# A two-layer cross-attention and expert kernel: first-layer experts on the whole array, second-attention scores in quarter arrays without spread queries, deeper rings for the scatters

## The reference

```python
x = x + xattn0(layernorm(x), ctx)            # 8 heads of 64, over the channels
x = x + ffn0(layernorm(x))                   # 16 experts, inner 64, top 2, and a shared expert
x = x + xattn1(layernorm(x), ctx, mask)      # 16 heads of 16
x = x + ffn1(layernorm(x))                   # 32 experts, inner 128, top 4

# ffn0, for the two chosen experts of a token
hmid = silu(x @ w1[e].T) * (x @ w3[e].T);   y += weight[e] * hmid @ w2[e].T
# xattn1
scores = clip(einsum('bhsd,bhtd->bhst', q, k) / 4, -50, 50)    # head h reads channels 16h to 16h+15
probs = softmax(where(mask, scores, -50));  ctx_ = probs @ v
delta = rs * (ctx_ @ Wo.T + bo);            delta = layernorm(delta) * gamma + beta
```

## Time and profile before

| what | value |
|---|---|
| its own time | 1966.79 us |
| its span in the trace | 1965.1 us |
| busy: PE, DVE, ACT, POOL | 1618.1, 1468.4, 1014.1, 1131.1 us |
| mean granted TensorE clock | 0.915 |
| attention 0 | 0 to 830 us |
| shared expert | 830 to 983 us |
| experts 0 | 983 to 1141 us |
| combine 0 | 1141 to 1176 us |
| attention 1 | 1176 to 1617 us |
| experts 1 | 1617 to 1899 us |
| combine 1 | 1899 to 1965 us |

### The profile page before, as it was taken

One profiled execution on the slowest core, in us unless ns is written; L12 is line 12 of the kernel. 1 busy time (PEld: TensorE's weight loads), 2 busy tenths in 40 slices (PEclk: granted clock), 3 DMA queues, 4 the chain that ended last, 5 costly groups with the idle time before them and its releaser, 6 DMA issues. The chain is left out here.

```text
span 1965.1 us, 44433 instructions
## 1 busy us (share of the span) xinstructions
PE 1618.1 (82%) x15032; PEld 1194.9 (61%) x15032; DVE 1468.4 (75%) x3211; ACT 1014.1 (52%) x3084; POOL 1131.1 (58%) x1061
## 2 busy tenths in 40 slices
PE   4999999999999999799477707988887209999958
PEld 3677777777777777566255403544445109999846
DVE  2799999999999999757244455999998407888767
ACT  2788888888888888534143303333332006655520
POOL 2566666666666666536445503568788544666543
PEclk9999999999999999989788858999897559999979
DMA  6400000000000000022344350011112544555438
GB/s 180 141 18 18 18 18 18 18 18 18 18 18 18 18 18 18 35 87 80 114 149 149 104 190 14 12 47 68 67 47 79 212 165 134 161 162 157 155 131 321
DMA packets 101070, 167.71 MB, mean 85 GB/s; under 512 B 19999, under 2 KB 75756, under 8 KB 100208
## 3 DMA queue, kind: packets, MB, share of 16 engines
q1 hardware_dynamic: 75120, 105.37, 16.9%
q0 software_dynamic: 22272, 56.15, 7.9%
q10 hardware_dynamic: 3456, 3.34, 0.5%
HBM read 95.31 MB, written 75.76 MB: 87 GB/s over the span
## 5 line engine op out<-in xcount | busy, mean ns | idle before, releaser
L380 POOL TENSOR_TENSOR w_down<-w_down,attn_rsum 128x1024 f32<-128x1024 f32 x256 | 484.7, 1893 | 287.8 <-DVE attn_rsum L336 287.7
L296 ACT ACTIVATE w_down<-attn_ps_s,attn_negmax 128x256 f32<-128x256 f32 x1024 | 469.8, 476 | 25.6 <-DVE attn_negmax L330 22.5
L852 POOL DMA_INDIRECT l_by_token<-l_experts_outs,l_experts_rows x240 | 244.8, 1020 | 198.4 <-issue 107.8
L330 DVE TENSOR_REDUCE attn_negmax<-attn_ps_s 128x4 f32<-128x1024 f32 x256 | 311.9, 1218 | 28.2 <-PE attn_ps_s L218 27.4
L341 DVE COPY w_down<-attn_ps_t 128x1024 f32<-128x1024 f32 x256 | 312.1, 1219 | 21.0 <-PE attn_ps_t L230 20.7
L218 PE MATMUL attn_ps_s<-ctx_d,attn_q_sb 64*128 64x256 f32 x2048 | 273.6, 379 | 1.6 <-ACT w_down L296 1.0
L244 PE MATMUL attn_ps_qo<-w_down,attn_vb 128*64 128x256 f32 x2048 | 249.3, 385 | 1.3 <-DVE w_down L341 1.3
L716 PE MATMUL l_experts_ps_gu<-l_experts_rows_t,l_experts_w_now 128*128 128x128 f32 (+1 forms) x1920 | 213.6, 290 | 30.4 <-issue 14.6
L218 PEld LDWEIGHTS attn_ps_s<-ctx_d,attn_q_sb 64*128 64x128 f32 x2048 | 223.8, 189 | 3.1 <-issue 2.2
L716 PEld LDWEIGHTS l_experts_ps_gu<-l_experts_rows_t,l_experts_w_now 128*128 128x128 f32 (+1 forms) x1920 | 194.3, 183 | 41.8 <-issue 41.8
L296 ACT ACTIVATION_READ_ACCUMULATOR w_down<-attn_ps_s,attn_negmax 128x1 f32 x1024 | 213.9, 209 | 0.0
(11 more groups left out here) (247 smaller groups left out, 2670.7 us busy)
## 6 DMA issues: line engine op xcount, KB each, us to landing
l_experts_rows<-l_rows_in SPq DMA_DIRECT2D x240, 136.0 KB
combine_rows_got<-l_by_token SPq DMA_DIRECT2D x32, 512.0 KB
ctx_d<-in_ctx SPq DMA_DIRECT2D x64, 128.0 KB
combine_rows_got<-l_by_token SPq DMA_DIRECT2D x32, 256.0 KB, 3.8
w_gu<-in_w_gu SPq DMA_DIRECT2D x2, 4096.0 KB, 17.9
l_rows_in<-zeros SPq DMA_DIRECT2D x1, 4352.0 KB, 39.6
x_sb<-in_x SPq DMA_DIRECT2D x32, 128.0 KB
w_down<-in_w_down SPq DMA_DIRECT2D x1, 4096.0 KB, 12.6
```

The lines of the kernel that those rows point to most:

```text
L296: last = nc.scalar.activation(prob[:, n % 4, c, :], ps_s[:, n % 2, c, :], ACT.Exp, bias=negmax[:, n % 2, c:c + 1], accum_out=sums[:, n % 2 ...
L330: nc.vector.tensor_reduce(negmax[:, n % 2, :], ps_s[:, n % 2, :, :], AX.X, ALU.max, negate=True).then_inc(max_ready, 1)
L380: nc.gpsimd.tensor_tensor(prob[:, n % 4, :, :], prob[:, n % 4, :, :], rsum[:, n % 2, :].unsqueeze(2).to_broadcast([P, 4, A_N]), ALU.mult). ...
L852: pool.indirect_dma_start(m.by_token, bass.IndirectOffsetOnAxis(ap=place, axis=0), outs[:, r % RING, b, :], None, bounds_check=T * m.K - 1 ...
```

## The change

**Experts 0.** Gate and up of a block come from one product of 128 columns (gate in columns 0 to 63, up in 64 to 127): four products a pair instead of eight. The silu reads the gate half and writes rows 64 to 127 of `glu`; DVE's product becomes two operations of 64 rows. `w_down0` gets a second copy with zeros in the other half, so that `down` contracts all 128 rows; `copy_down` and its semaphore go, and PE picks the expert by a register, as in layer 1. Two memsets of the zero halves are added to the setup.

**Attention 1.** The spreads of DVE and POOL (L1422) and the copies of the mask row (L1653) go. ACT makes, once per group and half f, four masked copies of the projected queries (`take_apart`, `q_apart`): copy h keeps head h of each 64-row strip. The scores of a tile are eight products of 64 rows by 64 columns, 256 query columns each, in quarters of the array. `q_t` is single-buffered; `xa` and `xt` get their own memory.

**Scatters.** `Routing.RING = 4`: slots, semaphores and `xf` are rings of four, in the shared stage the slots too. In attention 1 POOL's order by j is (g-3, k=1), (g-4, k=3), (g-2, k=0), (g-3, k=2), over 46 steps.

```diff
-                for u in range(2):
-                    if HALVES == 2:
...
+                for u in range(2 // HALVES):
+                    for b in range(2):
                         for kt in range(KT):
+                            last = nc.tensor.matmul(ps_gu[:, q % 2, u, b, :], w_now[:, q % 2, b, kt, u * P:(u + 1) * P],
+                                                    rows_t[:, q % 2, b, kt, :], start=(kt == 0), stop=(kt == KT - 1))
...
+                    weights = w_down[:, b, bass.ds(e[b], 1), :] if HALVES == 2 else w_down[:, bass.ds(e[b], 1), :]
...
-                if HALVES == 2 and 0 <= n + 1 < NP:
-                    copy_down(n + 1)
...
             def scores(it, r):
                 keys_ready(pe, it, r // GT)
-                tdone(pe, qbd0_ready, it, r)
-                tdone(pe, qbd1_ready, it, r)
+                gdone(pe, q_apart_ready, it, r // GT)
                 tdone(pe, clip_ready, it, r - 1)
                 for f in range(KT):
...
+                    for strip in range(2):
+                        rows = slice(strip * S, (strip + 1) * S)
+                        for b in range(2):
+                            t0 = (r % GT) * P + b * S
+                            last = nc.tensor.matmul(ps_s[b * S:(b + 1) * S, strip, f * 256:(f + 1) * 256],
+                                                    k_t[rows, (r // GT) % 2, f, t0:t0 + S],
+                                                    q_apart[rows, (r // GT) % 2, f, :, t0:t0 + S], start=True, stop=True)
...
+            def take_apart(it, q, f, u, heads_of_strip):
+                use_done(act, bank_free, it, u)
+                if q >= 2:
                     tdone(act, s_made, it, (q - 1) * GT - 1)
...
+                for h in heads_of_strip:
+                    last = nc.scalar.activation(q_apart[:, q % 2, f, h, :], q_t[:, f, :], ACT.Copy, scale=w["strip_mask"][:, h:h + 1])
...
-                if texists(it, r + 2):
-                    spread_queries(it, r + 2)
...
-                q = g - 2 if j >= 2 else g - 3
+                if j == 2 and gexists(it, g - 4):
+                    rt.mark_sent(pool, it, g - 4)
+                q, k = ((g - 3, 1), (g - 4, 3), (g - 2, 0), (g - 3, 2))[j]
```

More of the change, by code:

```diff
@@ L797, in clip @@
                 last.then_inc(gu_used, 1)
-            experts_of = block_experts(mybir.EngineType.DVE) if HALVES == 2 else None
-            def copy_down(n):
-                e = experts_of(0, n)
-                done(dve, y_made, 0, n - RING)
-                for b in range(2):
-                    last = nc.vector.tensor_copy(down_now[half(b), n % RING, :],
-                                                 w_down[half(b), bass.ds(e[b], 1), :].rearrange("p a n -> p (a n)"))
-                last.then_inc(down_ready, 1)
             def product(n):
@@ L812, in product @@
                 if bias is None:
-                    nc.vector.tensor_tensor(act_t[:, n % RING, 0, :], glu[:, n % 2, 0, :], ps_gu[:, n % 2, 1, 0, :], ALU.mult)\
-                        .then_inc(a_ready, 1)
+                    for b in range(2):
+                        last = nc.vector.tensor_tensor(act_t[half(b), n % RING, 0, :], glu[I:P, n % 2, b, :],
+                                                       ps_gu[I:P, n % 2, 0, b, :], ALU.mult)
+                    last.then_inc(a_ready, 1)
                 else:
@@ L889, in __init__ @@
         self.steps = ph.sem("routing_steps")
-        self.scattered = [ph.sem("scattered0"), ph.sem("scattered1")]
+        self.scattered = [ph.sem(f"scattered{n}") for n in range(Routing.RING)]
         self.rows_sent = ph.sem("rows_sent")
@@ L899 @@
     STEPS = 8
+    RING = 4
     def step_done(self, dve, it, q, n):
@@ L1415, in _ @@
                 sp.dma_start(into, source).then_inc(later_written, 16)
-        def block_diagonal(engine, it, r, f, ready):
-            t0 = (r % GT) * P
-            for b in range(2):
-                source = q_t[:, (r // GT) % 2, f, t0 + b * S:t0 + (b + 1) * S]
-                last = engine.tensor_tensor(q_bd[:, r % 2, f, b, :, :], source.unsqueeze(1).to_broadcast([P, C_HALF, S]),
-                                            w["head_mask"][:, :].unsqueeze(2).to_broadcast([P, C_HALF, S]), ALU.mult)
-            last.then_inc(ready, 1)
         @block.tensor
@@ L1549, in _, with copy_queries, copy_keys @@
             act.wait_ge(opened, 1)
[L1551 removed]
+            def copy_queries(it, q, f, u):
                 use_done(act, bank_made, it, u)
[L1553 to L1558 removed]
+                gdone(act, q_apart_ready, it, q - 1)
+                nc.scalar.activation(q_t[:, f, :], ps_q[:, :], ACT.Identity, bias=w["bq"][:, f:f + 1],
+                                     scale=C_DH ** -0.5).then_inc(bank_free, 1)
+            def take_apart(it, q, f, u, heads_of_strip):
+                use_done(act, bank_free, it, u)
+                if q >= 2:
+                    tdone(act, s_made, it, (q - 1) * GT - 1)
+                for h in heads_of_strip:
+                    last = nc.scalar.activation(q_apart[:, q % 2, f, h, :], q_t[:, f, :], ACT.Copy, scale=w["strip_mask"][:, h:h + 1])
+                if f == KT - 1 and heads_of_strip[-1] == 3:
+                    last.then_inc(q_apart_ready, 1)
+            def copy_keys(it, q, f, u):
+                use_done(act, bank_made, it, u)
+                if q >= 2:
+                    tdone(act, s_made, it, (q - 1) * GT - 1)
+                nc.scalar.activation(k_t[:, q % 2, f, :], ps_q[:, :], ACT.Identity, bias=w["bk"][:, f:f + 1])\
+                    .then_inc(bank_free, 1)
             def copy_values(it, r, u):
@@ L1614, in step @@
                         rt.exponentials(act, it, g - 2, gdone)
+                    if j == 1 and gexists(it, g + 1):
+                        take_apart(it, g + 1, f, u + 1 + f, (0, 1))
+                    if j == 2 and gexists(it, g + 1):
+                        take_apart(it, g + 1, f, value_use(r - 1) + 1 + f, (2, 3))
             copy_transposed(0, 0, xt, xa_t_made, xt_ready, xt_reader)
             for f in range(KT):
-                copy_projected(0, 0, f, f - 6, q_t, w["bq"], C_DH ** -0.5)
+                copy_queries(0, 0, f, f - 6)
+            for f in range(KT):
+                take_apart(0, 0, f, f - 6, (0, 1, 2, 3))
             act.wait_ge(prepared, 2)
@@ L1789, in _ @@
                 deviation(0, q, vare_a, rstd_a, steps_a, xa_ready, rstd_a_ready)
-            spread_queries(0, 0)
-            spread_queries(0, 1)
-            for r in range(NT + 2 * GT + 2):
+            rounds = [qk for g in range(NG + 5) for qk in ((g - 3, 1), (g - 4, 3), (g - 2, 0), (g - 3, 2)) if 0 <= qk[0] < NG]
+            for r in range(NT + 3 * GT + 2):
                 step(0, r)
-            rt.mark_sent(pool, NG // 2 - 1, 1)
+            rt.mark_sent(pool, 0, NG - 1)
         def counts_final(pe):
```

139 lines of the change are left out of this document (52 added, 87 removed).

## The result

The changed kernel took 1892.65 us, the median of four executions (1887.08 to 1900.79), against 1969.03 us before (1962.18 to 1975.22): a ratio of 0.9604, 95% interval 0.9570 to 0.9637, 76 us less. The profiled execution has a span of 1885.3 us against 1965.1, 79.8 less.

What follows compares the result with a forecast made beforehand. DVE was taken to bound attention 1, in lock-step with POOL. Attention 1 -54.5, tail -10, experts 0 +3, shared stage -1.5 make -63 on 1966.8, giving 1904; two thirds of 6.6 toward the median gives 1908 us, range 1886 to 1942.

Steps and rivals of the forecast that it cites:

- The forecast's floor: Full group of attention 1: DVE's work left without spreads and mask copies, its own short waits staying: 31.8 us.
- the lock-step of DVE and POOL: Full group of attention 1: the two meet every step, so the larger of each step counts, summing to 34.0 us.
- Groups 0 and 1: First two groups of attention 1: -3 us from halved scores in group 0, -5 us in group 1.
- rival (a): Attention 1: meeting points, masked copies or non-overlapping quarters bind; six groups save 3 to 6 us; 1925 to 1950 us; 22%.
- signs of being wrong: Scores still 1.9 us, PE waiting on ACT's copies, clock 0.5 in attention 1, or POOL always waiting while DVE idles.
- Rival (d): Attention 1: halved scores make PE less dense and its clock falls low; some +118 us, 2090 us; 4%, slower.
- The tail: POOL's scatter turns behind attention 1's last tile: 86 us becomes 76, taken as -10, bounds +5 and -20.
- the stall of 8: POOL's tail in attention 1: the 14.0 us stall shrinks to about 8 as other groups' turns fill it.
- The prologue: Attention 1 ahead of the first clip: eight masked copies on ACT, between 0 and +5.5 us, +3.5 taken.
- The term for `down`: Experts 0: `down` on 128 rows costs 0.43 us more a pair, 17 us if PE set the pace, 2 charged.
- rival (b): Attention 1: DVE's stretch goes too, DVE at 31 us a group, tail -20; total 1875 to 1895 us; 15%.
- the signs named: Right if full groups 33 to 36 us, DVE 28 to 30, PE 30 to 31, ACT 25, tail 76, experts 0 unchanged.

## Why the prediction was right, and where its steps were not

**What bounds the kernel.** Right. That PE isn't the bound is shown: with only PE relieved the groups stay at 43.1 us and the ratio at 0.9992. That it is DVE, and POOL only behind it, rests on their waits in the trace, not on a run that relieves one of them.

**DVE in a full group.** The forecast's floor, 31.8 us, is what came (31.9). It then raised this to 34.0 by the lock-step of DVE and POOL, taking the larger of the two in each step. That step failed: the run with 0.57 us more on POOL in each step shows that POOL's time is mostly not passed on, 3.0 us over all groups for 18 added, though in groups 3 and 5 most of it was. That the floor was met to 0.1 us is in part luck: it took DVE's 2.8 idle us as staying, they became 3.4, and DVE's busy time fell by 11.7 where 11.2 was counted. Groups 2 to 5 gave 43.0 for 36, 7 of the 17 us by which the forecast missed the profiled gain of 79.8.

**Groups 0 and 1.** -14.3 for -8. For PE, halving the scores (7.75 us to 4.38 in each) explains 3.4 a group; the quarters with spreads took only 1.4 off group 0 and nothing off group 1. Group 1 gained 9.0, of which quarters make 3.4 (the run with halves) and the spreads' end 5.6. The forecast had counted PE's busy time in these groups as work, and some of it went away with the spreads. By what way isn't shown.

**ACT.** Two errors that cancelled. The forecast counted sixteen masked copies a group, 11.0 us; four copies of each of two halves are eight, 5.3 us. And it costed them at nothing because of holes of 1.3 us. At its own count that would have been wrong: the run with ACT at 24.0 us a group, the load that the forecast wrote down (24.9), lost 45 us in the groups. The bound that the forecast gave for it, 5.6 us a group, is what that run measured in the mean; the working behind it, four times 1.4, is another, and a part of the loss is the clock's, so the equality is luck. Had the code had sixteen, a result like that run's is likely: its ratio, 0.988, makes 1945 of the 1969 us before, in the range of rival (a). A wait of PE on ACT's copies, one of the signs of being wrong, did come, 4.5 us in the prologue.

**PE and its clock.** Scores of a tile took 1.09 us for 0.97: the quarters run side by side, as assumed. PE in a full group is 28.8 us where 30.8 was forecast: the granted clock is 1.00 in groups 3 to 5, where the earlier trace rows has 0.88 for group 4. Rival (d) had it the other way: PE was to be less dense with less work. It became denser, since the groups shrank by 26% and PE's work by less: 28.8 of 31.9 is 0.90, against 35.6 of 43.0, 0.83, part of it at the lower level. With quarters alone PE did become less dense, and the clock of groups 3 to 5 was 0.87 in the mean for 0.92. The observation of the rival was right, its sign here was not.

**The tail.** -4.7 from the last beta addition to the last issue (86.4 to 81.7) for -10; within the bounds. Twelve turns came, as counted, and the stall of 8 was 7.5. The miss is in the turns, 5.6 us each where 5.4 was taken, and in the other waits for landings, 5.9 us where 3 was. The stall itself was put down to the turns' own order, and it is the 8 MB weight load: 7.5 us in the changed kernel, 14.0 in the old order with rings of two or four, 0.4 at most at that place with the load in pieces. That it shrank as forecast doesn't show the forecast's reason.

**The prologue.** +4.8 for +3.5: the eight copies take 4.99 us and PE waits for the values behind them.

**Experts 0.** +3 was forecast, the traces say -2.0, and the comparison of the two forms on one chip says 0. The term for `down`, 0.43 us a pair more, was right in size (48.4 us for 40 pairs where the kernel before has 32.0: 0.41 more) and is hidden. What failed is the share of it that a row buffer's round trip was to pay.

**Shared stage.** -2.5 for -1.5. The wait of DVE on `rows_sent` is gone; the profile has no such row in this stage.

In sum: the direction, the bound and the place were right. The result of 1892.65 lies below the 1895 to 1925 that had 54%, in the 1875 to 1895 of rival (b), though not for all of its reasons: the full groups (31.9 for its 31) and the outer ones went its way, its tail of -20 did not. That the whole range of 1886 to 1942 was met owes something to errors of opposite sign: the forecast of the groups was 14 us too careful, that of the tail 5 too bold, experts 0 off by 3 to 5, and 4.7 of the profiled gain belong to attention 0, which didn't change. Of the signs named, the scores in about 1 us, DVE's 28 to 30 us and experts 0 came; the full groups (31.9 for 33 to 36), PE (28.8 for 30 to 31), ACT (18.7 for 25) and the tail (81.7 for 76) did not.

## What to carry to other kernels

In the full groups here, the busy time of the bounding engine with its own short waits was the better forecast than the sum of the larger of two engines in each step; add for a second engine only what a trace or a run shows it to pass on. Where another engine sets the pace, as PE did in groups 0 and 1, this rule says nothing. Count what is put on an idle engine by the steps in which it lands and by what is queued behind it there: 5.3 us in two steps could be halved without any gain, 10.7 cost their excess in full, with the engine busy for 63% of the group. And when a stall behind a DMA's landing is at hand, look for a large transfer on the other queues first; cutting it in pieces and spreading them over the turns was worth 9.3 us of tail here, as much as the deeper rings and the best order of the turns together (86.3 to 77.4).

## What the runs showed of the hardware

From the first compute instruction of the stage to that of combine 0, experts 0 took 126 to 129 us on one chip, 153 to 156 on another, and 158 to 162 in the first comparison, either form of it on the first and the last; the whole kernel before was 1920.7 and 1921.8 us on the one against 1966.1 and 1969.0. This stage differed by a fifth to a quarter, while attention 0 ended at 823 to 826 us in all traces but that of the kernel before (828.5). The granted clock of the stage was 0.81 in the first two traces, 0.85 to 0.89 where it took 153 to 156 us, and 0.89 to 0.91 where it took 126 to 129; what makes the stage slower isn't shown.

Eight MB of plain transfers held the landing of 128-row scatters up for as long as 14 us, and while the same bytes came in 1 MB pieces, behind one turn each, no turn waited for a landing longer than 0.8 us. The 4.1 us before the very last turn remain, beside the stores of zeros; what held that landing up wasn't tried.
